# The recurrent stage written out unit by unit: fronts and tails between the units, keys and values spread by DMA, their product on GpSimd

## The reference

```
x = layernorm(x)
q, k, v = x @ Wq, x @ Wk, x @ Wv                  # reshaped to (b, t, 16 heads, 8)
gk = log_sigmoid(x @ Wg1 @ Wg2 + bg2) / 16
for t:  S = exp(gk_t)[..., None] * S + k_t[..., None] * v_t[..., None, :]     # an 8 x 8 state per head
        o_t = einsum('bhdv,bhd->bhv', S, q_t) * 8 ** -0.5
o = o * rsqrt(mean(o * o) + eps) * g_norm_w       # per head
g = x @ Wg
out = (o * g * sigmoid(g)) @ Wo                   # added to x
```

## Time and profile before

| | us |
|---|---|
| median of 3 runs | 3148.72 (3138.97 to 3154.59) |
| the profiled execution, its time | 3136.11 |
| its span (first to last instruction) | 3134.4 |
| the recurrent stage in it | 2381.0 to 2730.6, 349.6 us |

### The profile page before, as it was taken

One profiled execution on the slowest core, in us unless ns is written; L12 is line 12 of the kernel. 1 busy time (PEld: TensorE's weight loads), 2 busy tenths in 40 slices (PEclk: granted clock), 3 DMA queues, 4 the chain that ended last, 5 costly groups with the idle time before them and its releaser, 6 DMA issues. The chain is left out here.

```text
span 3134.4 us, 53202 instructions
## 1 busy us (share of the span) xinstructions
PE 2841.3 (91%) x19734; PEld 1636.1 (52%) x19734; DVE 2437.1 (78%) x3765; ACT 2216.7 (71%) x3896; POOL 190.3 (6%) x398
## 2 busy tenths in 40 slices
PE   6859999869999999969999899899997778899999
PEld 4644444423333333344444556788885445678887
DVE  6678999599999999578999454677776677778776
ACT  2357888759999999856888532488885444478887
POOL 0030000210000000030000110200000000010000
PEclk9968999979999999978999899899998888899999
DMA  1043220030000000043220110011112000011111
GB/s 30 0 127 69 42 41 4 10 107 22 22 22 22 22 22 12 2 126 69 42 32 12 38 47 1 24 45 48 45 48 69 1 0 0 1 41 55 55 48 47
DMA packets 76903, 115.24 MB, mean 37 GB/s; under 512 B 13905, under 2 KB 38513, under 8 KB 76657
## 3 DMA queue, kind: packets, MB, share of 16 engines
q1 hardware_dynamic: 76656, 111.99, 14.4%
HBM read 85.73 MB, written 25.43 MB: 35 GB/s over the span
## 5 line engine op out<-in xcount | busy, mean ns | idle before, releaser
L842 DVE TENSOR_REDUCE nested_a_halves<-banks 128x2 f32<-128x1024 f32 x512 | 613.1, 1221 | 72.7 <-PE banks L934 69.4
L889 ACT ACTIVATE nested_a_p<-banks 128x512 f32<-128x512 f32 x1024 | 552.6, 597 | 111.8 <-PE banks L964 87.0
L842 DVE TENSOR_REDUCE wide_a_halves<-banks 128x2 f32<-128x1024 f32 x512 | 593.7, 1217 | 33.5 <-PE banks L934 32.4
L889 ACT ACTIVATE wide_a_p<-banks 128x512 f32<-128x512 f32 x1024 | 553.9, 598 | 44.6 <-PE banks L964 33.1
L1781 DVE TENSOR_TENSOR mix_e_h_low<-mix_e_h,mix_e_h_high 128x512 fp32r<-128x512 f32 x512 | 350.4, 688 | 174.7 <-ACT mix_e_h_high L1910 167.3
L1925 ACT ACTIVATE mix_e_h<-banks,mix_b_folded 128x512 f32<-128x512 f32 x512 | 353.3, 690 | 108.0 <-PE banks L1987 107.7
L977 PE MATMUL banks<-nested_a_p,nested_values 128*32 128x256 f32 x4096 | 327.2, 398 | 0.0
L977 PE MATMUL banks<-wide_a_p,wide_values 128*32 128x256 f32 x4096 | 321.0, 391 | 0.0
L1910 ACT ACTIVATE mix_e_h_high<-mix_e_h 128x512 fp32r<-128x512 f32 x512 | 319.7, 625 | 0.0
L934 PE MATMUL banks<-nested_k_stack,nested_q_stack 48*128 48x512 f32 x1024 | 272.6, 527 | 41.3 <-DMA nested_q_stack<-nested_q_parts 21.8
L964 PE MATMUL banks<-nested_q_stack,nested_k_stack 50*128 50x512 f32 x1024 | 252.5, 422 | 11.1 <-ACT nested_a_p L889 10.3
(11 more groups left out here) (363 smaller groups left out, 4087.4 us busy)
## 6 DMA issues: line engine op xcount, KB each, us to landing
mix_e_gate<-mix_gates_t SPq DMA_DIRECT2D x128, 256.0 KB, 3.2
nested_q_stack<-nested_q_parts SPq DMA_DIRECT2D x96, 128.0 KB
nested_q_parts<-nested_q_cut SPq DMA_DIRECT2D x16, 512.0 KB
nested_k_parts<-nested_k_cut SPq DMA_DIRECT2D x16, 512.0 KB
nested_k_stack<-nested_k_parts SPq DMA_DIRECT2D x32, 256.0 KB
mix_raw_w<-L_ffn_w_t SPq DMA_DIRECT2D x16, 512.0 KB, 7.7
wide_q_stack<-wide_q_parts SPq DMA_DIRECT2D x192, 32.0 KB
nested_k_stack<-nested_k_parts SPq DMA_DIRECT2D x32, 128.0 KB
```

Of the source, the lines that this page charges most:

```text
L842: dve.tensor_reduce(halves[:, half, i, 2 * a:2 * a + 2], bank[:, at:at + 2, :], AX, ALU.max).then_inc(maxed, 1)
L889: act.activation(p[:, kt % 4, j, :], bank[:, ST + n % RING, :], ACT.Exp, scale=scale).then_inc(probs, 1)
```

## The change

- **Loop order.** `turns` and `Fori` are gone. Every engine runs one written-out loop `for u in range(64 + 11)`. With `i = u % 16`, the front of the next sequence and the tails of finished halves are placed at fixed values of `i`, between units, on each engine.
- **Spreading k and v.** ACT stores k and v to `k_t` and `v_t`; SP writes them to DRAM (two DMAs of 512 KB for a sequence) and reads them back spread over the state rows: three DMAs a unit (one of 256 KB for k, two of 128 KB for v) into rings of four (`k_p`, `v_p`). The matmuls and ACT's copy for them are gone, and DVE's cuts of q, k, v.
- **The product** k * v moves from DVE to POOL (`kv`, a ring of three), with both inputs in SBUF.
- **q and the decay** keep their two matmuls each. ACT writes the high part directly from PSUM, and DVE the rest; both are doubled, so that one sequence's can be made while the other's are read.
- PSUM: banks 6 and 7 are now `FRONT` (transposes and projections of the next sequence), 4 and 5 `GATHERED`, 2 and 3 `QUERY`, 1 `TAIL`, 0 `DECAY`.
- `ahead.load` is split: the small tensors at u = 16, the four groups of 1 MB at u = 24, 40, 48 and 56, all behind the spreads on SP.

```diff
-    def load(self, sp):
+    def load_small(self, sp):
...
+    def load_group(self, sp, g):
+        w = self.w
+        experts, chunks = self.rows(g)
+        sp.dma_start(self.w1[:, experts, :], ...).then_inc(self.w1_in[g], 16)
+        sp.dma_start(self.w2[:, chunks, :], ...).then_inc(self.w2_in[g], 16)
...
             def _(sp):
+                def store(b):
+                    for tile, dram, n in ((k_t, k_dram, K), (v_t, v_dram, V)):
+                        sp.wait_ge(kept, b * 8 + 2 * n + 2)
+                        wait_past(sp, outer, (b - 1) * UNITS)
+                        sp.dma_start(dram[b % 2], tile[:]).then_inc(stored, 16)
+                def spread(u):
+                    b, c, s, r = u // UNITS, u % UNITS // PAIRS, u % PAIRS, u % SPREADS
+                    wait_past(sp, outer, u - SPREADS + 1)
+                    rows = slice(2 * DH * s, 2 * DH * (s + 1))
+                    src = k_dram[b % 2, rows, half(c)].unsqueeze(1).broadcast_to([2 * DH, DH, BANK])
+                    sp.dma_start(k_p[:, r, :], src).then_inc(spread_in[r], 16)
+                    for j in range(2):
+                        rows = slice(DH * (2 * s + j), DH * (2 * s + j + 1))
+                        src = v_dram[b % 2, rows, half(c)].unsqueeze(0).broadcast_to([DH, DH, BANK])
+                        sp.dma_start(v_p[j * DH * DH:(j + 1) * DH * DH, r, :], src).then_inc(spread_in[r], 16)
...
-                ahead.load(sp)
+                store(0)
+                for u in range(ALL):
+                    b, i = u // UNITS, u % UNITS
+                    if i == 0:
+                        sp.wait_ge(stored, (b + 1) * 32)
+                    spread(u)
+                    if i == 13 and b + 1 < B:
+                        store(b + 1)
+                    if u == UNITS:
+                        ahead.load_small(sp)
+                    if i == 8 and b >= 1 or u == 3 * UNITS:
+                        ahead.load_group(sp, b - 1 if i == 8 else 3)
...
             def _(pool):
-                with pool.Fori(0, B) as it:
-                    front.on_gpsimd(pool, it)
+                ln.rstd_of(pool, 0)
+                for u in range(ALL):
+                    r, slot = u % SPREADS, u % PRODUCTS
+                    pool.wait_ge(spread_in[r], 48 * (u // SPREADS + 1))
+                    wait_past(pool, scanned, u - PRODUCTS + 1)
+                    pool.tensor_tensor(kv[:, slot, :], k_p[:, r, :], v_p[:, r, :], ALU.mult).then_inc(outer, 1)
+                    if u % UNITS == 0 and u // UNITS + 1 < B:
+                        wait_past(pool, front.normed, u // UNITS * TILES + TILES)
+                        ln.rstd_of(pool, u // UNITS + 1)
...
             def _(dve):
+                for u in range(ALL + 11):
+                    b, i = u // UNITS + 1, u % UNITS
+                    if u < ALL:
+                        scan(u)                       # waits outer, decay_copied
+                    if 1 <= u <= ALL:
+                        read_state(u - 1)             # waits q_spread
+                    for offset, part in ((5, 0), (7, 1), (10, 2)):
+                        n = tail_of(u, offset)        # the half n for which u == 8 * (n + 1) + offset
+                        if n is not None:
+                            tail(n, part)
+                    if b < B:
+                        if i == 0:
+                            ln.moments_of(dve, b)
+                        if i == 2:
+                            normalise(b)
+                        if i in (9, 11, 14):
+                            gate(b, (9, 11, 14).index(i))
+                        if i in (13, 14):
+                            rest_q(b, i - 13)
...
             def _(act):
+                for u in range(ALL + 11):
+                    b, i = u // UNITS + 1, u % UNITS
+                    if u < ALL:
+                        act.wait_ge(decay_spread, u + 1)
+                        wait_past(act, scanned, u - 1)
+                        act.activation(decay_p[:, u % 2, :], bank[:, DECAY, :], ACT.Copy).then_inc(decay_copied, 1)
+                    for offset, part in ((2, 0), (4, 1), (6, 2), (8, 3)):
+                        n = tail_of(u, offset)
+                        if n is not None:
+                            tail(n, part)
+                    if b < B:
+                        if i == 4:
+                            copy_turned(b)
+                        if i >= 6:
+                            keep(b, i - 6)            # z, k, v, q (high), silu: two halves each
+                        if i in (8, 9, 10, 12, 13):
+                            gate(b, (8, 9, 10, 12, 13).index(i))   # Abs, Exp, Ln, Exp, Copy
...
             def _(pe):
+                for u in range(ALL + 11):
+                    b, i = u // UNITS + 1, u % UNITS
+                    if u + 1 < ALL:
+                        spread(u + 1)                 # decay, then q, which waits read of unit u - 1
+                    if 1 <= u <= ALL:
+                        gather_unit(u - 1)
+                    for offset, part in ((3, 0), (8, 1), (9, 2)):
+                        n = tail_of(u, offset)
+                        if n is not None:
+                            tail(n, part)
+                    if b < B:
+                        if i == 3:
+                            turn_front(b)
+                        if 5 <= i <= 14:
+                            project(b, i - 5)         # waits that keep(b, i - 7) has emptied the bank
```

More of the change, by code:

```diff
@@ new lines, in _ @@
+                dve.wait_ge(folded, 1)
+                dve.tensor_copy(fold_g[:], bank[:, TAIL, 0:D]).then_inc(fold_copied, 1)
+                dve.wait_ge(made, 3)
+                for s in range(PAIRS):
+                    dve.tensor_copy(gather[:, s, 2 * DH * s:2 * DH * (s + 1)], same[:]).then_inc(made, 1)
+                gate(0, 0)
+                gate(0, 1)
+                for c in range(2):
+                    rest_q(0, c)
+                gate(0, 2)
+                for u in range(ALL + 11):
[17 more added lines that the diff above has]
+                            rest_q(b, i - 13)
@@ L2280, in _ @@
-                turns(act, B, turn)
+                act.wait_ge(w_in, 144)
+                copy_turned(0)
+                for n in range(2):
+                    keep(0, n)
+                for part in range(3):
+                    gate(0, part)
+                    if part == 0:
+                        for n in range(2, 6):
+                            keep(0, n)
+                for n in range(6, 8):
+                    keep(0, n)
+                for part in range(3, 5):
+                    gate(0, part)
@@ new lines, in _ @@
+                for n in range(8, 10):
+                    keep(0, n)
+                for u in range(ALL + 11):
[15 more added lines that the diff above has]
+                            gate(b, (8, 9, 10, 12, 13).index(i))
@@ new lines, in project @@
+                def project(b, n):
+                    kind, c = n // 2, n % 2
+                    at = FRONT + c
+                    if kind == Z:
+                        pe.wait_ge(front.copied, b * 2 + 2)
+                    elif kind == G:
+                        pe.wait_ge(q_rest, b * 2 + c + 1)
+                    else:
+                        pe.wait_ge(kept, b * 8 + n - 1)
+                    if kind == G:
+                        for i in range(4):
+                            last = pe.matmul(bank[:, at, i * P:(i + 1) * P], front.h_t[:, (4 * c + i) * P:(4 * c + i + 1) * P],
+                                             wg[:], start=True, stop=True)
+                    else:
+                        last = pe.matmul(bank[:, at, :], (fold_g, wk, wv, wq)[kind][:], front.h_t[:, half(c)],
+                                         start=True, stop=True)
+                    last.then_inc(projected, 1)
```

379 lines of the change are left out of this document (175 added, 204 removed).

## The result

The changed kernel takes 3113.9 us (median of 12 runs, 3099.1 to 3125.0) against 3141.9 for the kernel before (12 runs on the same chips): a ratio of 0.991, 95% interval 0.9891 to 0.993. It is 28 us faster, where 69 were forecast (3080). The profiled execution took 3110.7 us around a span of 3109.0, at a granted clock of 0.936.

The account below looks back on a forecast made before the run. PE bounds units now, a chain through all engines the gaps. Recurrent stage: 36 + 3 x 60.5 + 46 + 15 + 2 = 280.5 us against 349.6, 69 less; so 3080 us, range 3040 to 3118.

Parts of the forecast that it names:

- the chain behind a kept bank: Units i = 6 to 15: projection, ACT's keep, gate step, decay copy, scan, read; 2.83 + G/2 a unit, 37.5 us.
- Rival B: In-order lists stall more, from waits counted once per unit or the store's round trip: 3115 us, chance 0.24.
- i = 0: First unit of a sequence: POOL's power waits for DVE's moments, delaying the next product; 7.7 us in all.
- i = 2: Unit with the sum into x, normalise and a product between: 5.3 us.
- The product: POOL's multiplication of 512 columns: 1.2 us, bounds 1.0 and 1.5.
- The exclusion: DVE's scan and POOL's product lock each other out, the later waiting: 2.4 us a unit instead of 1.8.
- rival A: The scan isn't held up by POOL; 30 us more gain, 3050 us, chance 0.13.
- PE and DVE sums: Work a sequence in the recurrent stage: 44 us of PE, 45 us of DVE.
- DMA hidden: Spreads and store covered by issuing up to four units ahead: 0 us, upper bound 3 us a sequence.
- Clock: PE's clock above 0.9 over the units; 2 us in all for slower matmuls after pauses at i = 0.
- rival C: PE's clock falls to the 1.2 GHz level and the kernel becomes slower: 3190 us, chance 0.03.
- End: From the last unit's read to the stage's end, with the tail of half 6 before it: 15 us.

Follow-up runs that it names:

- The experiment: Changed kernel with GpSimd's layer-norm power moved behind the product of unit 2: 7.8 us off the stage, interval from unit 0 to 1 from 7.58 to 5.10.
- Short products: Changed kernel with POOL's product on 64 of 512 columns from the fourth unit on, computation incomplete: 11.3 us off the stage.
- the mends: Changed kernel with decay spread and copied two units ahead, power behind unit 2's product, store behind unit 15, own bank for last tail: 3063.0 us.

## Why the prediction was right in direction and wrong in size

- **The step that failed: the chain behind a kept bank, and the in-order list of ACT in it.** I took ten units as 37.5 us and six as 23. Sequence 1 has 48.2 and 26.5. The prediction let a decay copy wait for a keep and a gate step, and spread each such chain over two units, since PE projects one iteration before ACT keeps. It left out that ACT also waits for PE's transposes, with the decay copy behind. The copy of y and the square have transposes and copy in one iteration, so their chain closes in one unit: in sequence 1, 6.59 us at i = 8 and 6.98 at i = 12. The tail's middle stood in my sum as 3.5 us of DVE, and i = 7 with 5.77 us bears that out; on ACT nothing of the tail stood in the sum, and on PE not the tail's output matmuls, behind which a projection and its keep came late at i = 10 (7.11 us). That moving the copy alone gives 23.3 of the missing 41 us shows the order of ACT's list as the cause of that part.
- **Rival B** named this mechanism ("ACT copies the decay only one unit ahead") and gave 3115. Its mark was waits for the decay copy of over 60 us; they are some 62, of which the groups name 24. That its 3115 is so near the 3113.9 measured is in part luck, as it came from 8 to 10 us more in each of four sequences, and the missing time is spread otherwise. It deserved more than 0.24: I had counted those waits in the main case once a unit, from averages, and hadn't walked ACT's list through the eight tail units.
- **The missing 41 us by place:** sequences 2.7, 14.2, 16.0 and 6.5, the end 5.6 (20.6 from the end of the last scan, 15 forecast), less 1.6 of lead-in and the 2 set apart for the clock.
- **i = 0** was right: 7.7 forecast, 7.58 measured, with the wait for GpSimd's power as described. The experiment takes 2.5 of it away. **i = 2** was 5.62, 7.46 and 6.73, not 5.3: the sum into x waits for PE (17.5 us in all for eight).
- **The product:** 1.2 forecast, 1.26 at the least and 1.41 on average beside DVE. **The exclusion** was right as a mechanism and rival A is refuted: scans of up to 2.31 us where 1.22 and 1.28 are their length alone. The Trainium skill, "SBUF — State Buffer", section "Who interferes with whom", has the later of the two wait. The trace agrees: all 18 lengthened scans started behind a product under way and ended 1.08 us after it, and products get longer where they are the later ones. But 2.4 us was no floor: where GpSimd is ahead or late, units take 1.72. Short products gained 11.3 us of stage in the changed kernel, by one run.
- **PE and DVE sums** (44 and 45 us a sequence): PE 54.67 at a clock of 0.84, 45.9 at full clock; DVE 45.8 to 51.7 with 13 us of lengthened scans in all. Right. Two slips in the working change nothing: the ten units add up to 37.8 us, not 37.5, and DVE ended 0.54 us after GpSimd's 2747.83, not 0.64.
- **DMA hidden:** right (2.5 us in all, under the bound of 3 a sequence). The worst place was the store at i = 13 as described; GpSimd waited 11.16 us for the next unit's spread and the scan didn't notice. The sign of it was wrong: GpSimd's waits for spreads were not near zero elsewhere, but came before 24 of the 64 products, 90.4 us in all, 24.7 of them before the first and 29 at i = 14. The rows below are 40 slices of 0.25 us, 2590 to 2600, busy tenths of the DMA engines and GB/s. Sync issues a spread of k at 2590.05 and its two of v at 2590.63. In the first 1.5 us of the rows and again behind the burst 5 tenths are busy at 197 GB/s; in the burst that follows the issue of k it is 9 tenths at up to 336 GB/s.

```profile
DMA  5555557998654555552100000000000000000000
GB/s 197 197 197 197 205 188 295 336 229 156 131 82 98 188 197 197 205 197 107 41 25 25 25 25 25 16 0 0 0 0 0 0 0 0 0 0 0 0 0 0
```

- Half of 16 engines is eight. By the Trainium skill, "DMA: Bandwidth & Descriptors", section "Why a DMA increments its semaphore by 16 and not by 1", the copies of v, with eight rows outside, use eight engines. The busy share of 5 tenths fits that; which copy an engine was moving the rows don't say.
- **Clock:** 0.84 to 0.90 over the units, not above 0.9; rival C stayed far off. But the term of 2 us was too small, and it didn't stand at i = 0 alone. After some of the stalls PE's next matmuls had the 1.2 GHz level, and these stand in the chain behind the stall: from 2526.50 to 2529.30 the granted clock was 0.50, and in the 4.5 us before PE had been busy for 1.57.

```profile
2526.53 0.79 PE L2434 MATMUL banks<-rec_q_high,rec_pick 128*128 128x512 f32 x1 [1.22 <-DVE rec_q_state L2246]
...
2527.55 1.91 PE L2444 MATMUL banks<-rec_q_state,rec_gather 128*128 128x512 f32 x2
```

- Of the 64 gathers 15 took 1.5 us or more, where the others take about 1.02; together all 64 are some 14 us longer than that. With the decay copy one unit ahead 8 are, so part of its 23.3 us may be the clock's. How much of this lies on the path no run separates; it stays open.
- **Lead-in** 34.4 against 36. **End:** 20.6 us, not 15. The tail of half 6 stands before the last unit's read on DVE and its transposes before those of half 7:

```profile
2689.79 0.68 DVE L2246 TENSOR_TENSOR rec_q_state<-rec_state,banks 128x512 f32<-128x512 f32 x1
...
2692.39 1.06 PE L2458 MATMUL banks<-ident,rec_y 128*128 128x128 f32 x4
...
2695.34 0.69 DVE L2225 TENSOR_TENSOR x_resident<-x_resident,banks 128x512 f32<-128x512 f32 x1 [4.87 <-PE banks L2463]
2696.17 0.63 PE L2453 MATMUL banks<-ident,rec_o_t 128*128 128x128 f32 x4 [0.87 <-DVE x_resident L2225]
```

The stage that I had summed, 280.5 us, is near what the kernel reaches once the lists are mended (275.7): the loads were right, the order was not costed. That the two are so near is in part luck, since the mends also take out the stall at i = 0 that the sum had in it; with the copy two units ahead alone the stage is 290.7.

## What to carry to other kernels

When work is placed between the steps of a recurrence, walk each engine's list and write down what every placed instruction waits for; an instruction that waits for this iteration's result must stand behind the one that feeds the next iteration, not before it. A copy that feeds a recurrence wants to be the first entry of an iteration, one unit ahead. A wait of 90 us on an engine off the path says nothing until the path's own instruction waits for it, and it may begin to count (2.5, then 14.5 us) when the path gets shorter.

## What the runs showed of the hardware

Moving a product of 512 columns from DVE to GpSimd freed 42.7 us of DVE and changed the time by little: 10.1 us of stage in the changed kernel, none beyond chance with the mends (1.2 us the other way), as DVE's other instructions got 34.8 us longer beside GpSimd. Of a scan and a product the later one waits: scans that started under a product ended 1.08 us after it, with up to 2.31 us in place of 1.22 or 1.28, and a product beside DVE took up to 2.24 us, 1.26 alone.
